# Two gated-expert stages written out per unit: routing by four tiles between the units in layer 0, and layer 3's attention and experts as one program

## What is computed

```
# layer 0, feed-forward: 32 experts of width 96
probs = softmax(x @ gate_weight.T)                       # 32 per token
topv, topi = top_k(probs, 8); topv = topv / topv.sum()
active = topv * alpha >= 0.05  (or the largest, if none)
weights = topv * active, normalised to sum 1, placed by topi -> combine
out = sum over e of ((silu(x @ g_e) * (x @ u_e)) @ down_e) * combine[:, e]
# layer 3, attention: 16 query heads, 4 key heads of 128, rms-normed, softmax(q k^T) v @ Wo
# layer 3, feed-forward: 8 experts of width 176 (top 2 by softmax) and a shared one with weight 1
out = sum over e of combine[:, e] * ((silu(x @ w1_e) * (x @ w3_e)) @ w2_e) + shared
```

## Time and profile before

| | us |
|---|---|
| median of 3 runs | 1735.34 (1733.1 to 1735.41) |
| the profiled execution's own time | 1729.76 |
| its span, first to last instruction | 1727.6 |
| layer 0's expert stage, between barriers | 492.3 to 794.2 |
| layer 3's attention and expert stages | from 1308 to 1543, from 1543 to 1723 |
| mean granted clock | 0.94 |

### The profile page before, as it was taken

The page is one execution under the profiler, slowest core; times in us unless marked ns, Lnnn a source line. Parts: engine busy times, 40 slices in busy tenths (PEclk is TensorE's granted clock), DMA queues, the critical chain, the costliest instruction groups (busy, mean ns, idle before and its releaser), DMA issues. The chain is left out here.

```text
span 1727.6 us, 22490 instructions
## 1 busy us (share of the span) xinstructions
PE 1536.3 (89%) x6976; PEld 1061.8 (61%) x6976; DVE 921.8 (53%) x1997; ACT 730.0 (42%) x2045; POOL 515.8 (30%) x488
## 2 busy tenths in 40 slices
PE   3989998999977999998999999978556999979998
PEld 1667776777744555556788797744323666655554
DVE  7787889888744222223535445534674555533222
ACT  3878787888820111112344353332143555541110
POOL 3566578777620000002343342200001323320000
PEclk8999999999978999999999999986778999988999
DMA  4201000100053000001000000023110000000000
GB/s 177 105 4 56 4 4 28 48 1 1 1 226 132 0 0 1 0 1 56 1 1 1 1 16 11 0 92 122 48 50 1 1 1 1 1 2 1 0 0 25
DMA packets 8372, 52.75 MB, mean 31 GB/s; under 512 B 1717, under 2 KB 3781, under 8 KB 4928
## 3 DMA queue, kind: packets, MB, share of 16 engines
q1 hardware_dynamic: 7664, 50.50, 7.5%
q0 software_dynamic: 160, 0.68, 0.2%
q10 hardware_dynamic: 432, 0.15, 0.0%
HBM read 50.94 MB, written 1.05 MB: 30 GB/s over the span
## 5 line engine op out<-in xcount | busy, mean ns | idle before, releaser
L1147 DVE TENSOR_TENSOR l0f_hidden<-l0f_product,bank 128x512 f32<-128x512 f32 x48 | 33.0, 688 | 186.6 <-PE bank L1087 185.1
L1115 ACT ACTIVATE l0f_silu<-bank 128x512 f32<-128x512 f32 x48 | 28.7, 597 | 234.2 <-PE bank L1074 234.2
L823 POOL TENSOR_TENSOR l0a_stepped<-l0a_y,l0a_m 128x512 f32<-128x512 bf16 x64 | 76.1, 1190 | 108.0 <-DVE l0a_m L625 107.7
L845 POOL TENSOR_TENSOR l0a_head_rstd<-l0a_head_var,all_minus_half 128x4 f32<-128x4 f32 x96 | 100.6, 1051 | 12.8 <-DVE l0a_head_var L644 12.7
L1074 PE MATMUL bank<-l3f_xn_t,all_weights_b 128*128 128x512 f32 (+1 forms) x208 | 100.1, 627 | 2.9 <-DVE l3f_hidden L1147 2.9
L1074 PE MATMUL bank<-l0f_xn_t,all_weights_b 128*128 128x512 f32 x192 | 94.6, 616 | 0.9 <-DVE l0f_hidden L1147 0.9
L1097 PE MATMUL bank<-all_weights_a,l0f_hidden 128*128 128x256 f32 x384 | 91.6, 382 | 2.1 <-DVE all_x L1154 2.1
L776 ACT ACTIVATE l0a_work<-bank,l0a_neg_max 128x128 f32<-128x128 f32 x256 | 90.3, 369 | 5.7 <-DVE l0a_neg_max L657 5.6
L1074 PE MATMUL bank<-l0f_xn_t,all_weights_a 128*128 128x512 f32 x192 | 91.9, 601 | 0.0
L243 POOL TENSOR_TENSOR l1a_l1a_norm_rstd<-l1a_l1a_norm_var,all_minus_half 128x8 f32<-128x8 f32 x1 | 1.6, 1630 | 299.6 <-DVE l1a_l1a_norm_var L229 299.6
L1500 DVE TENSOR_TENSOR all_weights_a<-bank,all_cols 128x512 f32<-128x512 f32 x64 | 44.1, 691 | 85.8 <-PE bank L1357 85.7
(11 more groups left out here) (399 smaller groups left out, 3885.9 us busy)
## 6 DMA issues: line engine op xcount, KB each, us to landing
all_weights_a<-in_l_w_q SPq DMA_DIRECT2D x2, 2048.0 KB, 16.1
all_weights_b<-in_l_e_gate SPq DMA_DIRECT2D x1, 3072.0 KB, 10.3
all_weights_a<-in_l_e_up SPq DMA_DIRECT2D x1, 3072.0 KB, 13.1
all_weights_a<-in_l_e_down SPq DMA_DIRECT2D x1, 3072.0 KB, 20.1
all_weights_b<-in_l_w_qx SPq DMA_DIRECT2D x1, 2048.0 KB
all_weights_b<-in_l_w_proj_x SPq DMA_DIRECT2D x1, 2048.0 KB, 17.7
all_weights_b<-in_l_w_proj SPq DMA_DIRECT2D x1, 2048.0 KB, 9.0
all_weights_b<-in_l_w_q SPq DMA_DIRECT2D x1, 2048.0 KB
```

The costliest lines, as they stand in the source:

```text
L823: done = g.tensor_tensor(stepped[:, 0:n], value, step, ALU.add)
L845: g.tensor_tensor(head_rstd[:, m % 2, :], head_var[:, m % 2, :], res.minus_half[:, 0:HU], ALU.pow)\
```

## The change

`Signal` and `rotate` go. `gated_experts` becomes two programs, both written out by `march`, which existed before. The arithmetic of a unit stays: the same matmuls, silu and products, on the same shapes. Weights, `select` and placements stay as they are.

- **Layer 0** (`layer0_experts`): a step is a unit. `product` gets eight buffers (`DEEP = LAG + 1`, `LAG = 7`), and spread, weighing and down of unit n come 7, 7 and 8 steps after its up products. The gate and up banks are freed by `product`. There is one spread bank; the other, `late_bank`, serves logits and turns. Routing works on four tiles at a time and is cut into seven pieces, at steps 0 to 6 for the first half and 11 to 17 for the second. The second half's tiles are normed and turned at steps 0, 1, 8 and 9, two tiles per bank. POOL does its power in two halves, the first ahead of the load of `select`. SP loads `l0_e_up` in four pieces. `weight_t` is copied by ACT instead of DVE.
- **Layer 3** (`layer3`): attention and experts in one block. Steps 16 on also norm and turn attention's finished tiles for the experts (`F_VAR`, `F_ROWS`, `F_TURN`), the first half's routing is at steps 52 to 60, the up products of unit n at step 63+n, spread and `hidden` one step later, down seven steps later out of eight `hidden` buffers. The second half's routing is at steps 72 to 75. The turned tiles share `turn_bank` with the queries, so `turn` now also waits for `f_xn_ready`; `up_products` of unit n waits for silu and `hidden` of unit n-2. Each quarter of x is written out by its own DMA behind its addition.

```diff
-        product = mem.sb("product", [2, HALF])
+        product = mem.sb("product", [DEEP, HALF])
+    ROWS = [0, 1]
+    LOGITS = [0, 10]
+    SHIFT, SHARE, MEMBERS, SCALED, FALLBACK, ACTIVE, SPLIT = ([s, s + 11] for s in range(7))
+    TURN_WEIGHTS = [7, 18]
+    PAIRS = [8, 9]
...
+            def turn_weights(h):
+                pe.wait_ge(weight_ready, h + 1)
+                for t in range(4):
+                    mm = pe.transpose(late_bank[:, :].bitcast(BF16)[0:PARTS, t * P:(t + 1) * P],
...
+            def up_products(n, _):
...
+                product_done.wait(pe, product_done.at(n - 2, 1))
...
+            def spread_weights(n, _):
...
+                hidden_done.wait(pe, hidden_done.at(n - 1, 1))
+                pe.matmul(spread_bank[:], select[0:PARTS, j * P:(j + 1) * P], weight_t[0:PARTS, h * HALF:(h + 1) * HALF],
...
+            march(NF, 1, [(once(LOGITS, gate_logits), [0]), (up_products, [0]), (once(TURN_WEIGHTS, turn_weights), [0]),
+                          (once(PAIRS, turn_later), [0]), (spread_weights, [LAG]), (down_products, [LAG + 1])])
...
+            march(NF, 1, [(once(LOGITS, keep_logits), [0]), (once(SHIFT, exponentials), [0]), (silu_of, [0]),
+                          (once(TURN_WEIGHTS, keep_weights), [0]), (once(PAIRS, keep_later), [0])])
...
+            def multiply(n, _):
+                silu_done.wait(v, silu_done.at(n, 1))
+                v.tensor_tensor(product[:, n % DEEP, :], silu[:, n % 2, :], up_banks[n % 2][:], ALU.mult)\
...
+            def weigh(n, _):
+                spread.wait(v, spread.at(n, 1))
+                down_made.wait(v, down_made.at(n - 2, 1))
...
+            march(NF, 1, [(weigh, [LAG]), (once(SHIFT, shift_logits), [0]), (multiply, [0]),
+                          (once(ROWS, later_rows), [0]), (once(SHARE, share_probs), [0]),
+                          (once(MEMBERS, find_members), [0]), (once(SCALED, find_active), [0]),
+                          (once(FALLBACK, find_largest), [0]), (once(ACTIVE, add_fallback), [0]),
+                          (once(SPLIT, split_weights), [0]), (once([NCH - 1, NF - 1], add_to_x), [LAG + 1])])
...
-def layer3_attention(nc, top, res, w):
+def layer3(nc, top, res, w, out):
...
+    FIRST_UP = TILES * STEPS - 1
+    DOWN, DEEP = 7, 8
...
+    F_VAR = [(t + 2) * STEPS + 1 for t in range(TILES - 2)] + [65, 69]
+    F_ROWS = [(t + 2) * STEPS + 3 for t in range(TILES - 2)] + [66, 70]
+    F_TURN = [(t + 2) * STEPS + 4 for t in range(TILES - 2)] + [67, 71]
+    LOGITS = [F_TURN[4], 72]
+    SHIFT, SHARE, FIRST, SECOND, SPLIT = [53, 72], [54, 73], [55, 73], [56, 74], [57, 74]
+    TURN_WEIGHTS = [F_TURN[5], 75]
...
+        def _(sp):
+            for h in range(HALVES):
+                for k in range(2):
+                    f_x_done.wait(sp, f_x_done.at(h, k + 1))
+                    tiles = slice(4 * h + 2 * k, 4 * h + 2 * k + 2)
+                    sp.dma_start(out[:, tiles, :], res.x[:, tiles, :]).then_inc(written, 16)
...
+                if a == 2 and 2 <= b:
+                    f_xn_ready.wait(pe, f_xn_ready.at(b - 2, 1))
...
+                silu_done.wait(pe, silu_done.at(n - 2, 1))
+                hidden_done.wait(pe, hidden_done.at(n - 2, 1))
...
-            march(TILES, STEPS, [(score, later(UNIT, 2)), (turn_probs, later(UNIT, 4)), (turn, later(UNIT, 1)),
-                                 (mix, later(UNIT, 5)), (project, UNIT), (turn_rows, NORM),
-                                 (project_out, later(UNIT, 6))])
+            march(VTS, STEPS, [(attention(score), later(UNIT, 2)), (attention(turn_probs), later(UNIT, 4)),
+                               (attention(turn), later(UNIT, 1)), (attention(mix), later(UNIT, 5)),
+                               (attention(project), UNIT), (once(F_TURN, f_turn_rows), every),
+                               (once(LOGITS, gate_logits), every), (once(TURN_WEIGHTS, turn_weights), every),
+                               (attention(turn_rows), NORM), (attention(project_out), later(UNIT, 6)),
+                               (up_products, every), (spread_weights, later(every, 1)),
+                               (down_products, later(every, DOWN))])
...
+                               (once(SHIFT, gate_exponentials), every), (silu_of, every)])
...
+                               (once(SPLIT, split_weights), every), (multiply, later(every, 1)),
+                               (once(ADD, f_add_to_x), every)])
```

More of the change, by code:

```diff
@@ L1037, in gated_experts @@
[L1037 to L1043 removed]
+        var = mem.sb("var", [TILES])
+        rstd = mem.sb("rstd", [TILES])
@@ L1082, in spread_weights @@
+            def spread_weights(n, _):
+                h, j = divmod(n, NCH)
+                if n == 0:
                     pe.wait_ge(select_in, 16)
                 if j == 0:
[L1084 to L1088 removed]
@@ new lines, in split_weights, with multiply @@
+            def split_weights(h):
+                weight_turned.wait(v, weight_turned.at(h, 0))
+                for k in range(3):
+                    done = v.tensor_copy(weight_parts[:, :, k, :], weight[:])
+                    if k < 2:
+                        v.drain()
+                        v.tensor_tensor(weight[:], weight[:], weight_parts[:, :, k, :], ALU.subtract)
+                        v.drain()
+                done.then_inc(weight_ready.sem, 1)
+            def multiply(b, k):
+                n = chunk_at(b, k)
+                if n is None:
+                    return
+                m = CHUNKS[n % NCH][1]
+                silu_done.wait(v, silu_done.at(n, 1))
+                v.tensor_tensor(product[0:m, n % 2, :], silu[0:m, n % 2, :], up_banks[n % 2][0:m, :], ALU.mult)
+                v.drain()
+                spread.wait(v, spread.at(n, 1))
+                down_made.wait(v, down_made.at(n - DEEP, 1))
+                v.tensor_tensor(hidden[n % DEEP][0:m, :], product[0:m, n % 2, :], spread_bank[0:m, :], ALU.mult)                 .then_inc(hidden_done.sem, 1)
```

676 lines of the change are left out of this document (471 added, 205 removed).

## The result

The change made the kernel **45.7 us faster**: 1688.5 us (median of 4 runs, 1684.8 to 1689.9) against 1734.2 of the kernel before in the same session (4 runs), a ratio of 0.9743, 95% interval 0.9709 to 0.9777. The forecast was 1701 with a range of 1688 to 1716: the direction was right, the time lies at the edge of the range, and 11 of the 45.7 us were not foreseen.

A forecast was written before the change was run, and what follows sets the result against it. PE was taken as the bound (busy 1536 of 1728 us), with time to win only where it idles or runs slow. Layer 0's 17.7 and layer 3's 16.9 give 34.6 off 1735.3, so 1701 us, range 1688 to 1716.

The forecast's parts named there:

- (1): Layer 0 stage's start: shorter power, then transposes and logits of four tiles; first up product at 502.0, 5.9 us earlier.
- (2): Layer 0's first products: at 1.2 GHz for some 5.2 us, 2.6 us lost, same as before.
- (3): Layer 0 routing: 15 us per half instead of 20; PE stands 3.1 us, then a slow stretch costs 1.8.
- (4): Layer 0 between units: transposes 2.2, second logits 1.9, second turn of weights 0.3, together 4.4 us; table loads hidden.
- (5): Layer 0 change of halves: no cost, the 1.3 us addition fits behind up products; otherwise 2 us.
- (6): Layer 3 attention up to step 63: turns, logits, bank waits and routing add 10.7 us; at least 5.6, at most about 20.
- (7): Layer 3 from step 63: remaining work, turns, logits, three waits (3 us) and two slow ends (2 us); sum 166.3 us.
- (8): Layer 3's end: last quarter's DMA and barrier follow the addition; nothing won or lost, give or take 1.5 us.
- C (everything hides): Both stages: no wait at step 7, no slow ends, only 5.6 us added in attention; 1690 us, chance 0.13.
- A: Layer 0 routing still ends late, PE stands 4 us longer at step 7; near 1707 us, chance 0.12.
- D: Both stages slower: PE waits for the one spread bank in all 74 units; 1770 us, chance 0.03.
- B: Layer 3's merged stage stretches attention by 20 us, tiles over 2.5 us longer, 8 of waits later; 1715 us, chance 0.15.

The follow-up runs named there:

- the second look: The kernel after run once more, unchanged: 1684.6 us (5 runs), ratio 0.9712 to the kernel before.
- experiment 4: The kernel after with a lag of 2 units instead of 7 between product and weighing in layer 0: 1698.5 us, ratio 0.981.
- experiment 5: The kernel after with the last stage's first routing pieces moved to odd steps (53, 55, 55, 57, 59): 1686.5 us, ratio 0.9734.

## Why the prediction was right, and where it was short

The sign, the two places and most of the mechanism were right; 11 us of gain were missing in the medians, and 13 in the two stages. One reading was wrong from the start: a transpose is one instruction in the trace, and not two as the part on the kernel before says (the row of a pair of tiles in the earlier trace rows has four, and the code has four). The forecast counted each turn double. Point by point, against the profiled execution after:

- **(1) Start.** The first product comes 8.2 us behind the norm variance instead of 15.3: 7.1 won, 5.9 forecast. Power and sixteen logits took what the rows of before said (1.02, and 3.48 for 3.45). The missing 1.2 are the transposes: from the power's end to the start of the logits are 3.5 us, forecast 4.5 with eight transposes a pair where there are four.
- **(2) First clock.** Put at no change. The low clock ended at 505.5, 2.7 us behind the first product instead of the 5.2 of the earlier trace rows: 1.3 won here, nothing in the second look, where it ended at 507.9, 5.8 behind the first product.
- **(3) Routing.** Operations on half the columns took 0.29 (0.30 forecast). The last piece ended 38.4 us behind the variance; forecast 41.2, and the difference is the earlier start and the shorter low clock. The pieces take 13.5 us in one row (experiment 4), forecast 15. PE's stand was 2.55 instead of 3.1. The slow stretch of 1.8 behind it is **the term that failed in kind**: I took a chance event for a fixed price. It was absent in the first profile and there in the second, at 1.5.
- **(4) Added between the units** 2.8, not 4.4: a pair is four transposes of 0.11, and I had counted eight of 0.14 (1.3 us for the two pairs); the second logits take 1.70. The table loads are hidden, as forecast.
- **(5) Change of halves.** Nothing lost, as forecast. Last down product 768.1, or 273.5 us behind the variance where the forecast's own terms gave 279.5 (772.1 less the variance at 492.65). The terms as measured add up to 24.2 us for layer 0, within 0.7 of the stage's 23.5.
- **(6) Attention** 8.0 longer; forecast 10.7, bounds 5.6 to 20. The size was near by luck, for two errors cancel, and the place was wrong. (The terms as written add up to 10.6.) I spread 6.2 us of turns and waits over six tiles. In the trace a turn of a tile is two transposes, 0.22 and not 0.54, and lengthens its group by 0.16, from 6.64 to 6.80; the wait for the shared bank, 3 us in the sum, does not occur. Of the 8 us, 7.4 lie in the two last tiles: 1.9 the logits, 0.8 the group of the shares, 4.1 the group in which the piece stands ahead of the copy (2.5 of waiting and 1.7 of slow clock), 0.6 the last turn and the turn of weights. So the routing on DVE, put at 2, cost 4.9, about as much too little as the bank wait was too much.
- **(7) From step 63** 162.7 instead of 166.3: two waits of 0.87, not three of 1, and no slow ends (2 forecast); the two turns take 0.44, not 1.1.
- **(8) The end** 1.5 shorter: four DMAs of 256 KB land in 2.3 us each; I had no row of a store and took the 4.1 of a load for it, and set it to zero with the barrier.

Of the rivals, *C (everything hides)*, 1690, came closest by its number, with chance 0.13. Its conditions held in part: there is a short wait at the turn of weights and no slow end behind it, but attention has one, and (6) cost 8.0 and not 5.6. A and D did not occur: the first wait was 1.2 us, and units are 5.38 us throughout. Of B the sign occurred once, for the seventh tile is 6.8 us longer where 2.5 were the limit, but attention did not stretch by 20. The rule of the **Trainium skill** ("ScalarE: Activation LUTs", section "What ACT_TABLE_LOAD costs") of about 1.38 us of drain with each switch isn't borne out by these traces. The change of tables in unit 11:

```profile
558.40 0.31 ACT L1079 ACTIVATE l0f_probs<-l0f_logits 128x128 f32<-128x128 f32 x1 [4.98 <-DVE l0f_logits L1122]
558.73 1.28 ACT L1089 ACT_TABLE_LOAD   x1
560.02 0.60 ACT L1089 ACTIVATE l0f_silu<-bank 128x512 f32<-128x512 f32 x1
```

Exp ends at 558.71, the load fills 1.28, and silu starts 0.01 behind it: 1.3 us in all, and PE, which needs `product` 11 seven units later, never waits.

The range held, but barely, and that is in part luck: the first median lies 0.5 us inside it, the second look's 3 us below it. The large errors had the same sign. I counted each transpose twice, 4.8 us together (1.0 in (1), 1.3 in (4), 1.9 in (6), 0.6 in (7)), and waits that are covered and slow stretches that are a matter of chance as certain costs, 5.6 us in (3) and (7).

## What to carry to other kernels

Depth between two engines is worth the length of the detour it covers: eight buffers hid a routing of 13.5 us and won 13.7, and overlapping a chain-bound stage with a matmul-bound one won as much again. Before pricing instructions from a row, count them against the code: four transposes read as eight cost this forecast some 5 us. When work is laid into another engine's schedule, ask what stands next in that engine's order: in the last stage 1.8 us of small operations held up a copy for which PE waits, and the group grew by 4.1, or by 2.5 where the clock did not fall. And price a short stop of PE as an interval, from the stop alone to the stop and a slow stretch, because the same kernel draws either. A clock that falls or stays up can also pass for the gain of an edit, as 1.1 of the 1.9 us of experiment 5 did: compare with every profile that has the old order.

## What the runs showed of the hardware

- A stop of PE of about 2 us (waits of 1.20 and 0.77 around 0.26 of work) was followed by a group of products at half speed in three of nine profiles (3.38 to 3.49 us instead of 1.88) and by none in six, with the same waits. The three are those in which the clock rose late at the stage's start. Stages that no edit touched differed by up to 5.0 us between profiles (l1f 46.1 to 51.1) as the clock fell at other places. A gain of under 3 us is therefore better read from its stage than from the median, and from more than one profile, since the stage itself took 278.5 and 281.8.
- A DVE operation of 32 columns that takes 0.19 us takes 1.0 when it starts beside POOL's operation of 512 columns (1.04): it ends when POOL's does. The same happened to a conversion of 36 columns (0.99 instead of 0.19). Beside POOL's power of four columns (1495.02, 1.01 us) the same operations kept 0.19, and DVE's reductions that read a PSUM bank kept 0.69 in the eight groups of attention where they start beside POOL's scaling. The Trainium skill, page "SBUF — State Buffer", section "Who interferes with whom", says that a DVE instruction with two SBUF inputs contends with a GpSimd instruction that reads SBUF, and that the ports they share are an exclusive lock. For the scaling the trace agrees, with 1.05 for 0.19.
- The same kernel began its layer 0 stage with 2.7 us of products at the low clock in one execution and with 5.8 in another. The Trainium skill, page "TensorE: Matmul & The Clock Gate", Part 1, says that the number of slow products at a start varies between runs of one kernel; these two profiles agree.
- Products whose result nobody reads raised the clock ahead of real work: logits took 1.97 us instead of 3.62 behind eight of them. Behind four the clock fell again for one group in one profile (3.61 us) and stayed up in another (1.96).
